# The input projection of an attention and convolution kernel: float32 matmuls replaced by three f32r products of high and low parts

## The chip, the cores and the metric

One core of one Trainium2 chip runs the kernel. The metric is the device time in microseconds (us). Six names are used for the engines: PE (TensorE, matmul), PEld (its weight load), DVE (VectorE), ACT (ScalarE), POOL (GpSimd) and SP (SyncE, which issues the DMAs here).

## The reference, cut to what matters

```python
# x: (16, 512, 1024) f32; mask = cond_2048: (16, 1024) of 0 and 1; 8 heads of 64
q      = x^T @ Wq.T                                # (16, 1024, 512)
qh     = q split into 8 heads
scores = (1/8) * einsum('bhqd,bhkd->bhqk', qh, qh) # queries, keys and values are all qh
logits = (scores * cmask + (1 - cmask) * -1e30) * rmask
ctx    = softmax(logits) @ qh
x      = x + (ctx @ Wo.T)^T
x      = x + causal_depthwise_conv(x, taps = cond_2048) + bias
```

## The kernel before, in words

The attention goes batch by batch, 16 in all: batch 0 and batch 15 are written out ("first" and "last"), the 14 between are one hardware loop ("mid"). A batch is four pairs p of heads, a pair two heads i, a head eight steps t of 128 keys. The order is written by hand, engine by engine, with semaphores; on top of a step's own work a table (`MAX_AT`, `PROJ_AT`, `OUT_AT` and others) says which extra pieces a step carries.

**A step** of a head, (p, i, t): PE makes the scores of 128 keys against 1024 queries (L509 and L510, four matmuls into `sc`). ACT takes the exponentials in two halves (L627, into `p32`, two buffers) and rounds them to f32r (L629, `phi`, four buffers). POOL makes the remainder `plo = p32 - phi` (L699). PE multiplies `phi` and `plo` with the values two steps later (L523 and L527, six matmuls into `pv`). The scores of step t+1 wait for the exponentials of step t; the exponentials of step t wait for the `plo` of step t-2, since `p32` has two buffers; `phi` and `plo` wait for the products of step t-4.

**The extra pieces** share two banks `misc`: the maxima of the next head's scores (L471 on PE, L743 on DVE), their transpose `mneg` (L484, L763) at step 5, the values' transpose (L478, evicted by ACT L604) at step 6, the output projection of the batch before (L495, DVE L788), and the input projection. The last stands at steps 0 and 1 of a pair's first head and is for the next pair: at (3, 0) it is for pair 0 of the next batch. It multiplies `wq` and `xb`, both float32, over four blocks of 128 rows (L457); ACT evicts it twice (L593, `lo`; L594, `hi`), and DVE makes from it `mhi`, `lo` and `mlo` at steps 2 and 3 (L731, L726, L734). DVE normalises a pair at step 5 of the next pair's second head (`ct`, L779).

**The queue of SP** moves these rows to their places with DMAs (`operands`, `operands2`: L332), brings `mneg` as one row of 4 KB into `quer2` (`rows`: L362), and loads x. A head's first scores wait for its `mneg` row (`s_rows`). x and the mask of the next batch, 2 MB and 512 KB, are loaded by `load_x` (L323, L324), which waits for `s_masked`, that is `mlo` of the batch's last pair. In the kernel before the call stands at the beginning of head (2, 1):

```python
if phase != "last" and (p, i) == (2, 1):
    load_x(b + 1, pair(b, 3) + 1)
if i == 0 and not end:
    operands(*next_pair(b, p))
```

After the attention comes the convolution (L923 to L1014), which the change does not touch.

Of the kernel before, what the change touches and what calls it, by code (L numbers as in the profile page):

```python
# [15 lines left out]
P = 128  # L16
# [6 lines left out]
BAND = 96  # L23
NP32, NPHI, NPLO = 2, 4, 4
LAG = 2

# [89 lines left out]
class Prelude:  # L116
# [3 lines left out]
    def __init__(self, nc, ctx):  # L120
# [6 lines left out]
        with ExitStack() as place:  # L127
            self.keys = sb("keys", [P, 4, T], F32R, place)
            self.quer = sb("quer", [P, 4, T], F32R, place)
        self.xin = sb("xin0", [P, SLOTS, TH], F32)  # L130
        with ExitStack() as place:
# [3 lines left out]
        with ExitStack() as place:  # L135
            self.phi = sb("phi", [P, NPHI, T], F32R, place)
            self.plo = sb("plo", [P, NPLO, T], F32R, place)
            self.p32 = sb("p32", [P, NP32, T], F32, place)
        with ExitStack() as place:
# [4 lines left out]
        self.brow = sb("brow", [P, T], BF16)  # L144
        self.own = sb("own", [P, CH], F32)
        self.tri = sb("tri", [P, 2, CH], F32)
# [37 lines left out]
def build_attention(nc, x, cond, wqT, woT, x1, pre, taps_in, bias):  # L184


    with ExitStack() as ctx:  # L187
        def sb(name, shape, dt):
            return ctx.enter_context(nc.sbuf_tensor(name, shape, dt))

# [5 lines left out]

        wq = sb("wq", [P, DT, D], F32)
# [3 lines left out]
        xb = sb("xb", [P, DT, T], F32)  # L201
        mask = sb("mask", [P, T], F32)
# [9 lines left out]
        keys, quer, keys2, quer2 = pre.keys, pre.quer, pre.keys2, pre.quer2  # L212
        val = sb("val", [P, 2, KT, 2, P], F32R)
        mrow = sb("mrow", [P, KT], F32)
        mneg = sb("mneg", [KT, P], F32R)
        mask8r = sb("mask8r", [KT, P], F32R)
# [3 lines left out]
        ct = sb("ct", [P, PAIRS, T], F32)  # L220
        xo = sb("xo", [P, 2, T], F32)

# [7 lines left out]
        s_ident = sem("s_ident")  # L230
        s_x = sem("s_x")
        s_mask8 = sem("s_mask8")
        s_off8 = sem("s_off8")
# [76 lines left out]
        def tok(t):  # L310
            return slice(t * P, (t + 1) * P)

        x_v = x.rearrange("b (k p) t -> b p k t", p=P)
        cond_v = cond.rearrange("b (o t) -> b o t", o=1)
# [4 lines left out]
        def _(sp):  # L319
            def load_x(b, staged):  # L320
                if staged is not None:
                    sp.wait_ge(s_masked, staged)
                sp.dma_start(xb[:], x_v[b]).then_inc(s_x, 16)  # L323
                sp.dma_start(mask[:], cond_v[b].to_broadcast([P, T])).then_inc(s_x, 16)  # L324
# [49 lines left out]
            def start():  # L374
                for s in s_xo_out:
                    sp.sem_inc(s, 16)
                wq_v = wqT.rearrange("(k p) e -> p k e", p=P)
                sp.dma_start(wq[:, :, 0:P], wq_v[:, :, 0:P]).then_inc(s_begin, 16)
                sp.dma_start(xb[:, :, half(0)], x_v[0][:, :, half(0)]).then_inc(s_begin, 16)
                sp.dma_start(xb[:, :, half(1)], x_v[0][:, :, half(1)]).then_inc(s_x, 16)  # L380
                sp.dma_start(mask[:], cond_v[0].to_broadcast([P, T])).then_inc(s_x, 16)
                load_mask8(0, None)
                sp.dma_start(wq[:, :, P:D], wq_v[:, :, P:D]).then_inc(s_const, 16)
# [56 lines left out]
        def _(pe):  # L440
# [6 lines left out]
            def project(phase, b, p, step, h):  # L447

                out, full = take(phase, b, step, ("proj", h))
                out = out[:, 0:HALF]  # L450
                nb, np_ = (b, p) if phase == "start" else next_pair(b, p)
                if phase == "start":
                    pe.wait_ge(*((s_begin, 32) if h == 0 else (s_x, 32)))
                elif h == 0 and np_ == 0:
                    pe.wait_ge(s_x, 32 * nb + 32)
                for k in range(DT):
                    last = pe.matmul(out, wq[:, k, np_ * P:(np_ + 1) * P], xb[:, k, half(h)],  # L457
                                     start=(k == 0), stop=(k == DT - 1))
                last.then_inc(full, 1)
# [84 lines left out]
            def start():  # L544
# [3 lines left out]
                do("start", 0, 0, "head", PHASES["start"]["head"], (0, 0, 0))  # L548
                pe.wait_ge(s_const, 32)

# [31 lines left out]
        def _(act):  # L582
# [48 lines left out]
            def do(phase, b, p, step, items, nxt):  # L631
                for item in items:
                    if item[0] == "proj":
                        high_part(phase, b, p, step, item[1])
                    elif item[0] == "vt":
                        values(phase, b, step, item, nxt)

            def start():
                do("start", 0, 0, "pair", PHASES["start"]["pair"], None)
                do("start", 0, 0, "head", PHASES["start"]["head"], (0, 0, 0))  # L640

            def batch(phase, b):
                for p in range(PAIRS):
                    for i in range(2):
                        for t in range(KT):
                            first = phase == "first" and p == 0 and i == 0
                            exponentials(b, p, i, t, first)
                            if t == LAG - 1 and not first:
                                copy_context(*((b, p, 0) if i == 1 else (*before(b, p), 1)))
# [9 lines left out]
        def _(pool):  # L659
# [42 lines left out]
            def start():  # L702
                constants()
                masks()

            def batch(phase, b):
                for p in range(PAIRS):
                    for i in range(2):
                        for t in range(KT):
                            split(b, p, i, t, phase == "first" and p == 0 and i == 0)  # L710

            run(pool, start, batch, lambda: None)

        @block.vector
        def _(dve):
# [76 lines left out]
            def do(phase, b, p, step, items, nxt):  # L792
                for item in items:
# [4 lines left out]
                    elif item[0] == "out":  # L798
                        residual(phase, b, step, item, b - 1, item[1] + 1)

            def start():
                constants()
                table_masks()
                for parts in STAGE_AT.values():
                    for part in parts:
                        stage(0, 0, part)
                do("start", 0, 0, "head", PHASES["start"]["head"], (0, 0, 0))

            def batch(phase, b):
                for p in range(PAIRS):  # L810
                    for i in range(2):
                        for t in range(KT):
# [5 lines left out]
                            if not (phase == "first" and p == 0):  # L818
                                for part in REC_AT.get((i, t), []):
                                    reciprocals(*before(b, p), part)  # L820
                                if (i, t) == NORM_AT:
                                    normalise(*before(b, p))

            def table_masks():
# [240 lines left out]
```

## Time and profile before

| | us |
|---|---|
| median of 3 runs | 4283.91 |
| lowest and highest | 4280.56, 4286.85 |
| the profiled execution | 4281.65 |
| its span in the trace | 4279.9 |
| PE busy | 4128.9 (96%) |
| PE weight load busy | 2721.4 (64%) |
| ACT busy | 2849.9 (67%) |
| POOL busy | 2595.8 (61%) |
| DVE busy | 2491.4 (58%) |

The profile is of one execution. Busy times of PE are modelled at their ends, since matmuls overlap: the distance from start to start of neighbouring matmuls tells more of their price than the duration of one. PEclk is the granted clock of TensorE, 1.00 for 2.4 GHz and 0.5 for 1.2 GHz. A line number L is that of the kernel before. In a timeline "x4" means four instructions merged into one row, and the bracket at a row's end tells how long the engine was idle before it and who released it.

### The profile page before, as it was taken

The page shows a single profiled execution, that of the slowest core. Times are in us where ns is not written, and L with a number is a line of the kernel's source. Part 1 is how long each engine was busy: PE and PEld are TensorE (multiplying, and loading weights), DVE is VectorE, ACT ScalarE, POOL GpSimd, SP SyncE. Part 2 cuts the span into 40 slices and gives each one's busy share as a digit, 9 for nine tenths or more (in the row PEclk, how much of TensorE's full clock was granted, in tenths as well). Part 3 has the DMA queues.
Part 4 walks back from the last instruction along what each step waited for, and adds up shares of the span by engine and source line. Part 5 has one row for each costly group of instructions (what it writes and reads, how often), then busy time and mean ns, then how long its engine had stood idle before and what let it go on. Part 6 is the DMA issues. An engine that isn't in the chain of part 4 may idle for free. (4 is left out here: it accounts for less than half of the span.)

```text
span 4279.9 us, 56952 instructions
## 1 busy us (share of the span) xinstructions
PE 4128.9 (96%) x18688; PEld 2721.4 (64%) x18688; DVE 2491.4 (58%) x2260; ACT 2849.9 (67%) x3905; POOL 2595.8 (61%) x1044
## 2 busy tenths in 40 slices
PE   7999999999999999999999999999999999999799
PEld 4665666666566666656666665666666566666598
DVE  4664555556455655655565565656556565656576
ACT  4775767667576766757676675767667575767465
POOL 4775757667575766757576675757667575766300
PEclk8999999999999999999999999999999999999899
DMA  3323333232333333233333323333332332332488
GB/s 104 82 67 71 80 82 94 71 88 65 74 80 79 94 74 85 65 77 80 77 94 75 84 69 76 81 74 94 75 84 70 74 83 71 94 74 60 128 285 268
DMA packets 286191, 385.34 MB, mean 90 GB/s; under 512 B 148947, under 2 KB 217171, under 8 KB 285782
## 3 DMA queue, kind: packets, MB, share of 16 engines
q1 hardware_dynamic: 285910, 381.57, 34.9%
q8 instruction: 179, 2.93, 0.3%
q14 instruction: 102, 0.84, 0.1%
HBM read 112.28 MB, written 67.11 MB: 42 GB/s over the span
## 5 line engine op out<-in xcount | busy, mean ns | idle before, releaser
L699 POOL TENSOR_TENSOR plo<-p,phi 128x1024 fp32r<-128x1024 f32 x1024 | 2590.4, 2541 | 1404.1 <-ACT phi L629 1399.2
L743 DVE TENSOR_REDUCE mrow<-misc 128x1 f32<-128x1024 f32 x1024 | 1214.0, 1217 | 1067.5 <-PE misc L471 1067.5
L627 ACT ACTIVATE p<-sc 128x512 f32<-128x512 f32 x2048 | 1110.0, 594 | 855.2 <-PE sc L510 610.0
L523 PE MATMUL pv<-phi,val 128*128 128x512 f32 x4096 | 1192.3, 413 | 44.0 <-issue 44.0
L629 ACT ACTIVATE phi<-p 128x1024 fp32r<-128x1024 f32 x1024 | 1086.4, 1061 | 32.5
L523 PEld LDWEIGHTS pv<-phi,val 128*128 128x128 f32 x4096 | 724.1, 188 | 372.4 <-issue 226.0
L509 PE MATMUL sc<-quer,keys 128*128 128x512 f32 x2048 | 917.2, 448 | 23.5 <-issue 18.4
L510 PE MATMUL sc<-quer,keys 96*128 96x512 f32 x2048 | 808.6, 395 | 0.0
L527 PE MATMUL pv<-plo,val 128*128 128x512 f32 x2048 | 644.2, 395 | 0.7 <-POOL plo L699 0.7
L509 PEld LDWEIGHTS sc<-quer,keys 128*128 128x128 f32 x2048 | 386.7, 189 | 195.1 <-issue 75.7
L773 DVE RECIPROCAL den<-den 128x128 f32<-128x128 f32 x512 | 468.4, 935 | 50.2 <-ACT den L616 23.9
L495 PE MATMUL misc<-ct,wo 128*128 128x512 f32 x1024 | 466.9, 599 | 26.8 <-DVE mrow L743 18.9
L457 PE MATMUL misc<-xb,wq 128*128 128x512 f32 x1024 | 464.7, 597 | 8.7 <-DMA xb<-x 6.8
L510 PEld LDWEIGHTS sc<-quer,keys 96*128 96x128 f32 x2048 | 388.9, 190 | 112.0 <-issue 48.1
L471 PE MATMUL misc<-quer 64*128 64x512 f32 x2048 | 426.7, 465 | 25.0 <-DMA keys<-lo 11.7
L527 PEld LDWEIGHTS pv<-plo,val 128*128 128x128 f32 x2048 | 384.2, 188 | 93.5 <-POOL plo L699 1.4
L788 DVE TENSOR_TENSOR xo<-misc,xo 128x512 f32<-128x512 f32 x128 | 88.5, 691 | 450.8 <-PE misc L495 446.1
L471 PEld LDWEIGHTS misc<-quer 64*128 64x128 f32 x2048 | 167.3, 185 | 277.0 <-issue 244.2
L495 PEld LDWEIGHTS misc<-ct,wo 128*128 128x128 f32 x1024 | 189.7, 190 | 241.1 <-issue 204.6
L457 PEld LDWEIGHTS misc<-xb,wq 128*128 128x128 f32 x1024 | 195.3, 191 | 208.0 <-issue 187.0
L593 ACT ACTIVATE lo<-misc 128x512 f32<-128x512 f32 x128 | 76.6, 598 | 314.5 <-PE misc L457 314.5
L779 DVE TENSOR_TENSOR ct<-ca,den 128x1024 f32<-128x1024 f32 x63 | 205.4, 3260 | 13.9 <-DVE mneg L763 13.6
(67 smaller groups left out, 2647.7 us busy)
## 6 DMA issues: line engine op xcount, KB each, us to landing
keys<-hi SPq DMA_DIRECT2D x256, 256.0 KB, 3.1
quer<-mhi SPq DMA_DIRECT2D x256, 256.0 KB, 4.4
keys<-lo SPq DMA_DIRECT2D x128, 256.0 KB, 4.9
quer<-mlo SPq DMA_DIRECT2D x128, 256.0 KB, 3.8
xo<-x SPq DMA_DIRECT2D x64, 512.0 KB, 4.0
x<-xo SPq DMA_DIRECT2D x64, 512.0 KB, 5.1
xin<-x SPq DMA_DIRECT2D x16, 2048.0 KB, 13.6
out<-stage SPq DMA_DIRECT2D x64, 512.0 KB, 6.4
```

The source lines that it names most:

```text
L457: last = pe.matmul(out, wq[:, k, np_ * P:(np_ + 1) * P], xb[:, k, half(h)], start=(k == 0), stop=(k == DT - 1))
L471: last = pe.matmul(out[:, half(h)], quer[rows, k, tok(q)], quer[rows, k, half(h)], start=True, stop=True)
L495: last = pe.matmul(out, wo[:, k, m * P:(m + 1) * P], ct[:, k, half(h)], start=(k == 0), stop=(k == PAIRS - 1))
L509: pe.matmul(sc[:, h, :], keys[:, k, tok(t)], quer[:, k, half(h)], start=True, stop=False)
L510: pe.matmul(sc[:, h, :], keys2[:, i, tok(t)], quer2[:, i, half(h)], start=False, stop=True).then_inc(s_sc, 1)
L523: pe.matmul(pv[:, half(h)], val[:, i, t, part, :], phi[:, t % NPHI, half(h)], start=(t == 0 and part == 0), stop=False)
L527: last = pe.matmul(pv[:, half(h)], val[:, i, t, 0, :], plo[:, t % NPLO, half(h)], start=False, stop=(t == KT - 1))
L627: act.activation(p32[:, t % NP32, half(h)], sc[:, h, :], ACT.Exp, scale=SCALE).then_inc(s_p32, 1)
L629: act.activation(phi[:, t % NPHI, :], p32[:, t % NP32, :], ACT.Copy).then_inc(s_phi, 1)
L699: pool.tensor_tensor(plo[:, t % NPLO, :], p32[:, t % NP32, :], phi[:, t % NPHI, :].bitcast(F32), ALU.subtract).then_inc(s_plo, 1)
L743: reduced = dve.tensor_reduce(mrow[:, q:q + 1], misc[:, k, :], AX.X, ALU.max)
L773: dve.reciprocal(d, d).then_inc(s_rden, 1)
```

## The change

A float32 matmul of the input projection gives way to three f32r matmuls. The weights and x are split on the chip: ACT rounds a copy to f32r (`wqh`, `xh`), and the remainder is a subtraction (`wql`, `xl`). The projection is the sum `wqh*xh + wql*xh + wqh*xl`, twelve matmuls where the four float32 ones stood; the product of the two low parts is left out.

The weights are split at the start of the kernel. x of batch b+1 is split during head (2, 1) of batch b, in four blocks of 128x1024: ACT makes the high parts at steps 2, 3, 4 and 5, POOL the low parts of blocks 0 and 1 behind its `plo` of steps 4 and 6, DVE those of blocks 2 and 3 at steps 6 and 7. The projection at (3, 0) step 0 waits for all four. `load_x` is called at head (2, 0), after the `operands` of that head and ahead of `rows`. Some buffers change places in SBUF (`val`, `mneg` and `mask8r` move into the prelude's space, and the raw weights lie in `ct`).

```diff
+HI_AT = {2: 0, 3: 1, 4: 2, 5: 3}
+LO_POOL = {4: 0, 6: 1}
+LO_DVE = {6: [2], 7: [3]}
...
-                        if phase != "last" and (p, i) == (2, 1):
-                            load_x(b + 1, pair(b, 3) + 1)
                         if i == 0 and not end:
                             operands(*next_pair(b, p))
+                        if phase != "last" and (p, i) == (2, 0):
+                            load_x(b + 1, pair(b, 3) + 1)
                         if not (end and i == 1):
                             rows(nb, np_, ni)
...
                 if phase == "start":
-                    pe.wait_ge(*((s_begin, 32) if h == 0 else (s_x, 32)))
+                    if h == 0:
+                        pe.wait_ge(s_wql, 1)
+                    pe.wait_ge(s_xl, h + 1)
                 elif h == 0 and np_ == 0:
-                    pe.wait_ge(s_x, 32 * nb + 32)
-                for k in range(DT):
-                    last = pe.matmul(out, wq[:, k, np_ * P:(np_ + 1) * P], xb[:, k, half(h)],
-                                     start=(k == 0), stop=(k == DT - 1))
+                    pe.wait_ge(s_xl, split_done(nb, 2, 2))
+                    pe.wait_ge(s_xl_pool, 2 * nb)
+                cols = slice(np_ * P, (np_ + 1) * P)
+                for n, (w, xs) in enumerate(((wqh, xh), (wql, xh), (wqh, xl))):
+                    for k in range(DT):
+                        last = pe.matmul(out, w[:, k, cols], xs[:, k, half(h)],
+                                         start=(n == 0 and k == 0), stop=(n == 2 and k == DT - 1))
...
+            def input_high(b, k):
+
+                if k == 0:
+                    act.wait_ge(s_x, 32 * b + 32)
+                act.activation(xh[:, k, :], x32[:, k, :], ACT.Copy).then_inc(s_xh, 1)
...
             def start():
+                act.wait_ge(s_begin, 32)
+                act.activation(wqh[:, :, 0:P], wq32[:, :, 0:P], ACT.Copy).then_inc(s_wqh, 1)
+                act.activation(xh[:, :, half(0)], x32[:, :, half(0)], ACT.Copy).then_inc(s_xh, 1)
+                act.wait_ge(s_x, 32)
+                act.activation(xh[:, :, half(1)], x32[:, :, half(1)], ACT.Copy).then_inc(s_xh, 1)
...
+            def input_low(b, k):
+
+                pool.wait_ge(s_xh, split_done(b, DT, k + 1))
+                pool.tensor_tensor(xl[:, k, :], x32[:, k, :], xh[:, k, :].bitcast(F32), ALU.subtract).then_inc(s_xl_pool, 1)
...
+            def first_low(h):
+
+                dve.wait_ge(s_xh, h + 1)
+                dve.tensor_tensor(xl[:, :, half(h)], x32[:, :, half(h)], xh[:, :, half(h)].bitcast(F32), ALU.subtract).then_inc(s_xl, 1)
```

Three places show how the order moves. The first is SP's queue in head (2, 0) of the loop, from the last operand rows of pair 3 on. Before:

```order
L332 DMA keys<-lo 64x1024 x2
L361 REGISTER_ALU
L362 DMA quer<-mneg 1x8x128
L370 REGISTER_ALU
L371 ISA
L371 DMA x<-xo 128x16x64
L350 ISA
L332 DMA keys<-hi 64x1024
L332 DMA quer<-mlo 64x1024
L323 ISA
L323 DMA xb<-x 128x4x1024
```

And of the change (L383 is the `mneg` row, L344 and L345 the load):

```order
L353 DMA keys<-lo 64x1024 x2
L344 ISA
L344 DMA x<-x 128x4x1024
L345 ISA
L345 DMA mask<-cond 128x1024
L382 REGISTER_ALU
L383 DMA quer<-mneg 1x8x128
L391 REGISTER_ALU
L392 ISA
L392 DMA x<-xo 128x16x64
```

The load of x and the mask now stand ahead of the `mneg` row of head (2, 1) in the same queue, where they stood behind it.

The second place is POOL in head (2, 1) of the change, from step 4 to step 7 (L741 is the `plo` of a step, L751 the low part of x); before, only the `plo` stood there:

```order
L741 TENSOR_TENSOR plo<-p,phi 128x1024
L750 ISA
L751 TENSOR_TENSOR xl<-x,xh 128x1024
L738 REGISTER_ALU
L741 TENSOR_TENSOR plo<-p,phi 128x1024
L738 REGISTER_ALU
L741 TENSOR_TENSOR plo<-p,phi 128x1024
L750 REGISTER_ALU
L751 TENSOR_TENSOR xl<-x,xh 128x1024
L738 REGISTER_ALU
L741 TENSOR_TENSOR plo<-p,phi 128x1024
```

Between the `plo` of step 4 and that of step 7 POOL now has four instructions where it had two.

The third place is DVE in the same head, from step 5 on (L812 is `mneg`, L828 is `ct`, L863 the low part of x, L792 a maximum of the head after):

```order
L812 SCALAR_TENSOR_TENSOR mneg<-misc,mask 8x128
L827 REGISTER_ALU
L828 TENSOR_TENSOR ct<-ca,den 128x1024
L862 REGISTER_ALU
L863 TENSOR_TENSOR xl<-x,xh 128x1024
L862 REGISTER_ALU
L863 TENSOR_TENSOR xl<-x,xh 128x1024
L789 REGISTER_ALU
L792 TENSOR_REDUCE mrow<-misc 128x1 x2
```

Two subtractions over two SBUF operands now follow `ct`, where the next head's maxima followed it.

## Rows read from the trace of the kernel before

**Rows 1.** The page: busy time of each engine, its share of the span

```profile
PE 4128.9 (96%) x18688; PEld 2721.4 (64%) x18688; DVE 2491.4 (58%) x2260; ACT 2849.9 (67%) x3905; POOL 2595.8 (61%) x1044
```

**Rows 2.** The attention as one stretch: us, busy of PE, PEld, DVE, ACT, POOL, PEclk

```profile
40.00:3930.00 3890.00, 3796.35 (x15098) 2442.91 (x15099) 2238.13 (x2018) 2647.89 (x3628) 2531.53 (x1001) 1.00 0.32 78
```

**Rows 3.** PE in order of time: start us, us, line; float32, then f32r matmuls

```profile
2074.79 3.60 PE L457 MATMUL misc<-xb,wq 128*128 128x512 f32 x8
2078.23 3.60 PE L495 MATMUL misc<-ct,wo 128*128 128x512 f32 x8
...
2173.29 0.39 PE L509 MATMUL sc<-quer,keys 128*128 128x512 f32 x1
...
2174.22 1.09 PE L523 MATMUL pv<-phi,val 128*128 128x512 f32 x4
```

**Rows 4.** A group of the page: the input projection

```profile
L457 PE MATMUL misc<-xb,wq 128*128 128x512 f32 x1024 | 464.7, 597 | 8.7 <-DMA xb<-x 6.8
```

**Rows 5.** The line of the load of x: count, first and last start

```profile
L323 SPq DMA_DIRECT2D xb<-x x15: 455/460/632, 188.3 to 3676.6; - x15
```

**Rows 6.** ACT in head (2, 1), in order of time: phi of step 2, exponentials of step 3

```profile
2191.20 1.06 ACT L629 ACTIVATE phi<-p 128x1024 fp32r<-128x1024 f32 x1
2192.28 1.08 ACT L627 ACTIVATE p<-sc 128x512 f32<-128x512 f32 x2
```

**Rows 7.** POOL, in order of time, in heads (2, 0) and (2, 1)

```profile
2168.08 13.91 POOL L699 TENSOR_TENSOR plo<-p,phi 128x1024 fp32r<-128x1024 f32 x5 [4.38 <-ACT phi L629]
...
2192.42 4.75 POOL L699 TENSOR_TENSOR plo<-p,phi 128x1024 fp32r<-128x1024 f32 x2 [2.19 <-ACT phi L629]
...
2200.69 5.76 POOL L699 TENSOR_TENSOR plo<-p,phi 128x1024 fp32r<-128x1024 f32 x2 [0.79 <-ACT phi L629]
```

**Rows 8.** DVE at the same times: lo, mlo and ct

```profile
2168.02 1.22 DVE L726 TENSOR_TENSOR lo<-lo,hi 128x1024 fp32r<-128x1024 f32 x1
...
2170.29 2.28 DVE L734 TENSOR_TENSOR mlo<-lo,mask 128x1024 fp32r<-128x1024 f32 x1
...
2200.92 3.25 DVE L779 TENSOR_TENSOR ct<-ca,den 128x1024 f32<-128x1024 f32 x1 [0.23 <-DVE mneg L763]
```

**Rows 9.** PE: the first scores of head (2, 1), the projection at (3, 0)

```profile
2181.33 0.50 PE L509 MATMUL sc<-quer,keys 128*128 128x512 f32 x1
...
2208.77 3.59 PE L457 MATMUL misc<-xb,wq 128*128 128x512 f32 x8
```

**Rows 10.** SP's queue in head (2, 0)

```profile
2171.26 2.34 SPq L332 DMA_DIRECT2D keys<-lo  x2
2176.23 0.71 SPq L362 DMA_DIRECT2D quer<-mneg  x1
```

**Rows 11.** Stretches of 1 and 6 us: busy per engine, PEclk, DMA share, GB/s

```profile
2176.00:2177.00 1.00, 1.00 (x6) 0.77 (x5) 0.85 (x2) 0.97 (x2) 1.00 (x1) 1.00 0.22 41
2184.00:2190.00 6.00, 5.33 (x24) 3.35 (x22) 6.00 (x7) 5.05 (x6) 5.82 (x3) 1.00 0.98 396
```

**Rows 12.** Start of the kernel, DMA issues: KB each, median us to landing

```profile
wq<-wqT SPq DMA_DIRECT2D x1, 768.0 KB, 9.2
```

**Rows 13.** Start of the kernel, in order of time

```profile
3.81 0.40 SPq L383 DMA_DIRECT2D wq<-wqT  x1
...
6.85 8.71 PE L457 MATMUL misc<-xb,wq 128*128 128x512 f32 x16 [6.85 <-DMA xb<-x]
...
39.30 0.63 SPq L362 DMA_DIRECT2D quer<-mneg  x1
...
41.19 0.76 PE L509 MATMUL sc<-quer,keys 128*128 128x512 f32 x1 [3.44 <-DMA quer<-mneg]
```

**Rows 14.** The tail of the attention, PE after an idle stretch, in order of time

```profile
3982.51 1.47 PE L523 MATMUL pv<-phi,val 128*128 128x512 f32 x4 [2.17 <-issue]
```

**Rows 15.** The stretch right after it: busy per engine, PEclk, DMA share, GB/s

```profile
3983.00:3987.00 4.00, 4.00 (x12) 3.13 (x12) 0.00 (x0) 2.60 (x5) 3.21 (x2) 0.57 0.00 0
```

**Rows 16.** A wait of PE in one batch, 1932 to 2181 us: total, times, longest

```profile
PE sc L509 <- issue: 1.4, 1, 1.4
```

More of the change, by code:

```diff
@@ L129, in __init__ @@
             self.quer = sb("quer", [P, 4, T], F32R, place)
+            self.mneg = sb("mneg", [KT, P], F32R, place)
+            self.mask8r = sb("mask8r", [KT, P], F32R, place)
         self.xin = sb("xin0", [P, SLOTS, TH], F32)
@@ L187, in build_attention, with sb @@
     with ExitStack() as ctx:
-        def sb(name, shape, dt):
-            return ctx.enter_context(nc.sbuf_tensor(name, shape, dt))
+        def sb(name, shape, dt, where=ctx):
+            return where.enter_context(nc.sbuf_tensor(name, shape, dt))
         def ps(name, shape):
@@ L200, in build_attention @@
         ident = ident_r[:].bitcast(F32)
-        xb = sb("xb", [P, DT, T], F32)
+        xh = sb("xh", [P, DT, T], F32R)
+        with ExitStack() as place:
+            x32 = sb("x32", [P, DT, T], F32, place)
+        xl = sb("xl", [P, DT, T], F32R)
         mask = sb("mask", [P, T], F32)
@@ L212, in build_attention @@
         keys, quer, keys2, quer2 = pre.keys, pre.quer, pre.keys2, pre.quer2
-        val = sb("val", [P, 2, KT, 2, P], F32R)
+        val = pre.val
         mrow = sb("mrow", [P, KT], F32)
-        mneg = sb("mneg", [KT, P], F32R)
-        mask8r = sb("mask8r", [KT, P], F32R)
+        mneg, mask8r = pre.mneg, pre.mask8r
         p32, phi, plo = pre.p32, pre.phi, pre.plo
@@ L231, in build_attention @@
         s_x = sem("s_x")
+        s_wq = sem("s_wq")
+        s_wqh = sem("s_wqh")
+        s_wql = sem("s_wql")
+        s_xh = sem("s_xh")
+        s_xl_pool = sem("s_xl_pool")
+        s_xl = sem("s_xl")
         s_mask8 = sem("s_mask8")
@@ L311, in tok, with split_done @@
             return slice(t * P, (t + 1) * P)
+        def split_done(b, per, of):
+            return 2 + per * (b - 1) + of
         x_v = x.rearrange("b (k p) t -> b p k t", p=P)
@@ L647, in batch @@
                             exponentials(b, p, i, t, first)
+                            if phase != "last" and (p, i) == (2, 1) and t in HI_AT:
+                                input_high(b + 1, HI_AT[t])
                             if t == LAG - 1 and not first:
@@ L710, in batch @@
                             split(b, p, i, t, phase == "first" and p == 0 and i == 0)
+                            if phase != "last" and (p, i) == (2, 1) and t in LO_POOL:
+                                input_low(b + 1, LO_POOL[t])
             run(pool, start, batch, lambda: None)
@@ L799, in do, with weights_low, input_low @@
                         residual(phase, b, step, item, b - 1, item[1] + 1)
+            def weights_low(part, cols):
+                dve.wait_ge(s_wqh, part + 1)
+                dve.tensor_tensor(wql[:, :, cols], wq32[:, :, cols], wqh[:, :, cols].bitcast(F32), ALU.subtract).then_inc(s_wql, 1)
+            def first_low(h):
+                dve.wait_ge(s_xh, h + 1)
+                dve.tensor_tensor(xl[:, :, half(h)], x32[:, :, half(h)], xh[:, :, half(h)].bitcast(F32), ALU.subtract).then_inc(s_xl, 1)
+            def input_low(b, k):
+                dve.wait_ge(s_xh, split_done(b, DT, k + 1))
+                dve.tensor_tensor(xl[:, k, :], x32[:, k, :], xh[:, k, :].bitcast(F32), ALU.subtract).then_inc(s_xl, 1)
             def start():
@@ L803, in start @@
                 table_masks()
+                weights_low(0, slice(0, P))
+                first_low(0)
+                first_low(1)
                 for parts in STAGE_AT.values():
@@ L822, in batch @@
                                     normalise(*before(b, p))
+                            if phase != "last" and (p, i) == (2, 1):
+                                for k in LO_DVE.get(t, []):
+                                    input_low(b + 1, k)
             def table_masks():
```

24 lines of the change are left out of this document (16 added, 8 removed).

## The prediction

> **What bounds the kernel now.** I read the busy times of the page first, then the attention as one stretch, then PE in order of time, then one batch in the places that the change touches. The page has PE at 96% and no other engine above 67% [rows 1]. In the stretch of the attention PE is busy 3796 of 3890 us [rows 2], so a matmul taken away there shortens the kernel, as long as nobody else is late. Busy time alone could mislead, since PE's durations overlap; so look at starts. Four f32r matmuls of 512 columns go from 2173.29 to 2174.22, that is 0.2325 us each. The eight instructions of one projection (four float32 matmuls, each counted twice) stand 3.44 us before what follows them [rows 3]. PE really is full, and the steps show which others could become late: the scores of a step wait for exponentials, these wait for `plo` two steps back, and POOL makes that.
>
> **What the change takes from PE.** A projection becomes 12 x 0.2325 = 2.79 us, 0.65 less. There are 1024 / 8 = 128 projections [rows 4], two of them at the start, before the stream of work is full. The other 126 give 126 x 0.645 = 81.3 us, all on the path if the other engines keep up. The shape and kind are those of the rows, so this price is firm; at 0.25 us a matmul, more than the four of the row take, the gain would be 55 us.
>
> **The splitting of x, 15 times** [rows 5]. Take the batch whose head (2, 1) begins at 2181 us. *ACT*: `phi` of step 2 ends at 2192.3. A copy of 1024 columns costs what `phi` costs, 1.06, and the exponentials of a step 1.08 [rows 6]. With a copy behind each step, the high part of block 0 ends at 2193.3, step 3 with its copy at 2196.5, and `phi` of step 4 is ready at 2198.7. *POOL and DVE*: here the rows show something that the busy shares hide. DVE's subtraction takes 1.22 us alone, but `mlo` took 2.28 and `ct` 3.25 [rows 8]; and POOL's `plo`, 2.37 in an undisturbed pair, took 13.91 for five over `lo` and `mlo`, and 5.76 for two over `ct` [rows 7]. So a DVE instruction with two SBUF operands and a POOL one don't run together: each waits for the other, and every such meeting costs POOL 5.76 - 4.75 = 1.0 us. From 2198.7 these two therefore have one queue: `plo` 4, low part of block 0, `ct`, `plo` 5, low part 2, `plo` 6, low part 3, low part of block 1. That is 5 x 2.37 + 3 x 1.0 = 14.9 us, to 2213.6, plus 0.2 for the semaphore. The projection at (3, 0), which must wait for the low parts, began at 2208.77 [rows 9]. It is 5.0 us late, whatever order the two engines take in between: `plo` 5 is late too and holds up exponentials and PE at step 7, but inside the same 5 us. Nothing later gives it back, since PE is then the bound again. 15 x 5.0 = **75 us**. Bounds: were the meetings free, the queue is 11.9 us and the delay about 2; were every wait of step 7 in addition, 7.
>
> **The load, moved by half a head.** Before, the load stood behind the `mneg` row of head (2, 1); now it is ahead of it, issued at about 2173.6 when `keys<-lo` has been issued, where `mneg` comes at 2176.23 [rows 10]. Do DMAs of this queue overtake each other? At the start 768 KB were issued at 3.81 [rows 13] and landed 9.2 us later [rows 12]; at the 396 GB/s of a load under way [rows 11] 768 KB take 2 us. They waited for what was ahead of them. I take it that 4 KB wait as well. The operand rows ahead drain until about 2176.2 (the DMA share falls to 0.22 in that microsecond [rows 11]). 2.62 MB then take 6.3 to 6.6 us, and with 0.4 to the semaphore the row lands at about 2183.1, where the first scores of head (2, 1) started at 2181.33 [rows 9]. That is 1.8 us of idle PE, 15 x 1.8 = **27 us**. Bounds: 0 if small transfers pass (the row lands 1.9 us after its issue on an empty queue, 39.30 to 41.19 [rows 13]), 3 if the load is slow to start. All of the head shifts, so this adds to the 5.0.
>
> **The start.** PE's first projection began at 6.85 [rows 13], on landing. Now ACT must copy 512 columns and then 2048 (0.6 + 2.0 by its 1.06 for 1024), DVE subtract 2048 (2 x 1.22): PE begins at 11.8. Before, 16 instructions took 8.71 where 16 x 0.43 = 6.9 would do, so 1.8 us went to the low clock; 24 x 0.2325 + 1.8 = 7.4, to 19.2 instead of 15.56: **+3.7 us**. The split of the remaining weights (1536 columns, 1.4 on ACT and 1.8 on DVE) falls where DVE idles for the operand rows, and costs nothing; without that cover it would be 1.8, once. The changed SBUF places cost nothing that a row could show.
>
> **The clock.** In the tail PE was idle for 2.17 us, and in the 4 us after it the granted clock was 0.57 [rows 14, 15]; four matmuls then lasted 1.47 where they last 1.09 at full clock [rows 3]. At half rate for most of 4 us that is 1.7 us lost. In the loop no idle stretch was that long (the longest of a batch is 1.4 us [rows 16]), and there the clock stayed at 1.00 [rows 2]. Now PE idles 2 to 4 us in head (2, 1) and before (3, 0). Part of the slow stretch lies under the wait for the low parts, so I take 1 us of the 0 to 1.7: **+15 us**. The Trainium skill (TensorE: Matmul & The Clock Gate, "HAM oscillation — how this bites in real kernels") speaks of the same danger, a clock that falls in each wait between groups of matmuls and is paid every time; by it the sum would have the full 1.7, 26 us, and by the loop of the trace alone 0.
>
> **The sum.** 4281.65 - 81.3 + 75 + 27 + 3.7 + 15 = 4321. The profiled execution is 2.3 us below the median, so I say **4323**. A measurement of this kernel can tell 0.2%, 8.6 us, from no change; this is 0.9% slower.
>
> **Rivals.**
> *Faster: the cover holds.* PE's 81 us are certain, and both costs are worked out from queues. If the meetings of POOL and DVE don't add up in that head (the delay is then the 2 us of the lower bound) and small rows pass the load, the time is 4281.65 - 81 + 30 + 4 = 4234, with the median 4237; with the DMA wait as forecast, 4264. For it: POOL is 61% busy and idles whenever projections run. Against it: the extra work sits in steps 4 to 7, the steps without projections, where POOL has `plo` every 2.4 us. It decides at a delay of 3.7 us per batch, both waits together. Chance 0.18.
> *No change: no DMA wait and no fall of the clock.* The 5.0 stay: 4281.65 - 81.3 + 75 + 3.7 = 4279, with the median 4281. For it: the load might reach the engines before the operand rows have drained. Chance 0.12.
> *Much slower: the clock.* If it falls after each of the two waits of a batch and neither slow stretch lies under a wait, that is 15 x 3.4 = 51 instead of 15: 4357, with the median 4359. For it the row of the tail, and beside it the skill's section named above. Against it: the idle stretches of the loop, up to 1.4 us, never did it. Chance 0.12.
> *The change does not do what it says*, that is, x comes no earlier: excluded by the order rows, the load is three DMAs earlier.
> The forecast has 0.58. Its own range is 4300 to 4345.
>
> **How the numbers follow.** Slower by over 0.2%: 0.58 + 0.12 = 0.70. Within: 0.12. Faster: 0.18. The range reaches down to 4258, taking in no change and the milder half of the faster case, and up to 4355, which leaves out the rest of the clock case.
>
> **What would show it.** Right: projections of 2.8 us; in each batch but the last, PE idle 1.5 to 2 us at the start of head (2, 1), put down to the `mneg` DMA; PE waiting for `plo` at step 7, and the projection at (3, 0) waiting for POOL's or DVE's `xl`, 5 us in all; the distance from load to load 249 to 251 us, where it was (3676.6 - 188.3) / 14 = 249.2 [rows 5]; PE busy down by some 80 us, idle up by more. The steps are wrong if the scores of (2, 1) start without a wait (then the order of the queue), if `plo` in steps 4 to 7 keeps its 2.4 us beside the low parts (then the shared queue of POOL and DVE), or if the granted clock stays at 1.00 through the loop (then the 15 us).

## The result and the profile after

The changed kernel takes 4365.93 us (median; 4350.04 to 4366.11), the kernel before, run beside it, 4283.86 (4280.56 to 4286.85). The ratio is 1.018, with an interval from 1.0166 to 1.0194: 1.8% slower, where 0.9% was forecast. The profiled execution took 4350.04. It is the shortest of them, so what the trace shows may be up to 16 us short. A fourth execution took 10689.9 us; it is left out of the range and the ratio, and without it the median is 4365.75.

The page of the changed kernel, the line of busy times, beside [rows 1]:

```profile
PE 4092.9 (94%) x19200; PEld 2841.2 (65%) x19200; DVE 2599.0 (60%) x2294; ACT 2909.8 (67%) x3969; POOL 2701.4 (62%) x1074
```

PE is busy 36 us less in a kernel that is 68 us longer (4350.04 against the 4281.65 of the execution profiled before). The work was taken away, and idle time and slow time came in. The groups of the changed lines, beside [rows 4]:

```profile
L741 POOL TENSOR_TENSOR plo<-p,phi 128x1024 fp32r<-128x1024 f32 x1024 | 2612.4, 2562 | 1366.9 <-ACT phi L656 1360.8 <-PE pv L553 3.1
L483 PE MATMUL misc<-xh,wqh 128*128 128x512 f32 x512 | 142.8, 401 | 42.5 <-POOL xl L751 28.9 <-DVE xl L858 11.7 <-DVE mrow L792 1.9
L863 DVE TENSOR_TENSOR xl<-x,xh 128x1024 fp32r<-128x1024 f32 x30 | 100.7, 3396 | 0.0
L751 POOL TENSOR_TENSOR xl<-x,xh 128x1024 fp32r<-128x1024 f32 x30 | 86.1, 2869 | 0.0
L669 ACT ACTIVATE xh<-x 128x1024 fp32r<-128x1024 f32 x60 | 62.5, 1042 | 0.0
```

DVE's low part takes 3.40 us on average, where the same subtraction alone takes 1.22 [rows 8]; POOL's takes 2.87 where 2.37 is its own price [rows 7]. The waits of PE name the places:

```profile
PE sc L535 <- DMA quer<-mneg: 54.1, 15, 5.1
PE misc L483 <- POOL xl L751: 28.9, 15, 2.6
PE pv L553 <- POOL plo L741: 19.2, 16, 1.3
PE misc L483 <- DVE xl L858: 11.7, 1, 11.7
```

The first three have 15 or 16 places each, about one per batch, and are 102 us together. Of the first row 3.4 us are the wait at the start of the kernel, which was there before [rows 13]; the other 51 are new, 3.6 us in each of 14 batches (in batch 0 PE stands idle for 1.8 us at this point, which the profile puts down to "issue"). The fourth row is the start. The distance from one load of x to the next is now (3734.0 - 180.1) / 14 = 253.9 us, where it was 249.2 [rows 5]:

```profile
L344 SPq DMA_DIRECT2D x<-x x15: 375/438/524, 180.1 to 3734.0; - x15
```

Now one batch in order of time. SP's queue, which answers to [rows 10]:

```profile
2206.03 2.34 SPq L353 DMA_DIRECT2D keys<-lo  x2
2208.57 0.43 SPq L344 DMA_DIRECT2D x<-x  x1
2209.18 1.01 SPq L345 DMA_DIRECT2D mask<-cond  x1
2210.88 0.71 SPq L383 DMA_DIRECT2D quer<-mneg  x1
```

The row is issued 2.3 us after the load that stands ahead of it. PE at the start of head (2, 1), which answers to the first row of [rows 9]:

```profile
2215.34 0.62 PE L553 MATMUL pv<-plo,val 128*128 128x512 f32 x2
2218.94 0.79 PE L535 MATMUL sc<-quer,keys 128*128 128x512 f32 x1 [2.97 <-DMA quer<-mneg]
2219.52 0.63 PE L536 MATMUL sc<-quer,keys 96*128 96x512 f32 x1
...
2222.08 2.07 PE L549 MATMUL pv<-phi,val 128*128 128x512 f32 x4
2223.95 1.05 PE L553 MATMUL pv<-plo,val 128*128 128x512 f32 x2
2224.81 0.63 PE L535 MATMUL sc<-quer,keys 128*128 128x512 f32 x1
...
2247.66 0.50 PE L535 MATMUL sc<-quer,keys 128*128 128x512 f32 x1
```

PE begins 8.1 us after the row's issue, having idled for 2.97. Then four matmuls last 2.07 us where they last 1.09 at full clock [rows 3], and scores of two matmuls stand 0.43 apart (2219.52 to 2219.95 in the trace), not 0.23. The stretches around it (us, busy of PE, PEld, DVE, ACT, POOL, PEclk, DMA share, GB/s) show what the clock did:

```profile
2211.00:2217.00 6.00, 4.97 (x27) 3.78 (x25) 2.58 (x3) 5.49 (x8) 5.67 (x3) 1.00 0.98 369
2217.00:2219.00 2.00, 0.06 (x1) 0.07 (x1) 0.00 (x0) 0.56 (x1) 1.36 (x1) 0.89 1.13 336
2219.00:2225.00 6.00, 6.00 (x15) 3.93 (x16) 3.21 (x3) 2.25 (x3) 3.10 (x2) 0.50 0.65 128
2225.00:2250.00 25.00, 22.94 (x102) 15.68 (x101) 19.61 (x14) 21.31 (x28) 18.63 (x8) 0.99 0.10 22
```

In this batch PE works for 6 us at 1.2 GHz, the lower of its two levels, after 3 us of idling, and then at 2.4 GHz again. The end of the head, from the wait for `plo` at step 7 to the projection at (3, 0), which answers to the second row of [rows 9]:

```profile
2246.93 0.73 PE L553 MATMUL pv<-plo,val 128*128 128x512 f32 x2 [1.23 <-POOL plo L741]
...
2253.56 1.20 PE L483 MATMUL misc<-xh,wqh 128*128 128x512 f32 x4 [2.43 <-POOL xl L751]
2254.59 1.07 PE L483 MATMUL misc<-xh,wql 128*128 128x512 f32 x4
2255.50 1.08 PE L483 MATMUL misc<-xl,wqh 128*128 128x512 f32 x4
2256.42 0.39 PE L535 MATMUL sc<-quer,keys 128*128 128x512 f32 x1
```

The projection now takes 2256.42 - 2253.56 = 2.86 us where it took 3.44 [rows 3], but it stands 34.6 us behind the head's first scores where it stood 27.4 [rows 9]. POOL in the 13 us before it, beside [rows 7]:

```profile
2241.18 2.40 POOL L751 TENSOR_TENSOR xl<-x,xh 128x1024 fp32r<-128x1024 f32 x1
2243.54 6.68 POOL L741 TENSOR_TENSOR plo<-p,phi 128x1024 fp32r<-128x1024 f32 x2
2250.18 3.33 POOL L751 TENSOR_TENSOR xl<-x,xh 128x1024 fp32r<-128x1024 f32 x1
```

And DVE at the same times, beside [rows 8]:

```profile
2241.32 3.34 DVE L828 TENSOR_TENSOR ct<-ca,den 128x1024 f32<-128x1024 f32 x1 [0.23 <-DVE mneg L812]
2244.58 6.72 DVE L863 TENSOR_TENSOR xl<-x,xh 128x1024 fp32r<-128x1024 f32 x2
2251.22 2.34 DVE L792 TENSOR_REDUCE mrow<-misc 128x1 f32<-128x1024 f32 x2
```

The two take turns: POOL's instructions stand 3.3 us apart, 1.0 more than its own 2.37, and DVE's 3.35, which is a POOL instruction and its own work. The start, beside [rows 13]:

```profile
11.69 2.05 PE L483 MATMUL misc<-xh,wqh 128*128 128x512 f32 x4 [11.69 <-DVE xl L858]
...
45.48 0.77 PE L535 MATMUL sc<-quer,keys 128*128 128x512 f32 x1 [3.45 <-DMA quer<-mneg]
```

PE begins 4.8 us later, and the first scores are 4.3 us later than before.

So the trace holds all that was forecast, and more of it. Three questions stay for experiments: what each part costs by itself, since 82 us of loss are the small difference of large terms; whether the position of the load alone does what the wait says; and whether the full projection can be had without its costs.

### The profile page after: what moved, and what is told of

The parts are those of the page before. It is cut to its first block and busy times, and to the rows that moved or that the text cites. A ratio compares the mean times of both kernels' runs of the same rounds, so it can differ in the third digit from the quotient of the medians.

```text
span 4348.3 us, 58190 instructions
## 1 busy us (share of the span) xinstructions
PE 4092.9 (94%) x19200; PEld 2841.2 (65%) x19200; DVE 2599.0 (60%) x2294; ACT 2909.8 (67%) x3969; POOL 2701.4 (62%) x1074
## 5 line engine op out<-in xcount | busy, mean ns | idle before, releaser
L741 POOL TENSOR_TENSOR plo<-p,phi 128x1024 fp32r<-128x1024 f32 x1024 | 2612.4, 2562 | 1366.9 <-ACT phi L656 1360.8
L792 DVE TENSOR_REDUCE mrow<-misc 128x1 f32<-128x1024 f32 x1024 | 1213.5, 1216 | 1043.6 <-PE misc L497 1043.6
L549 PE MATMUL pv<-phi,val 128*128 128x512 f32 x4096 | 1212.0, 418 | 43.6 <-issue 43.6
L549 PEld LDWEIGHTS pv<-phi,val 128*128 128x128 f32 x4096 | 736.1, 191 | 382.2 <-issue 234.3
L535 PE MATMUL sc<-quer,keys 128*128 128x512 f32 x2048 | 877.8, 429 | 75.7 <-DMA quer<-mneg 54.1
L553 PE MATMUL pv<-plo,val 128*128 128x512 f32 x2048 | 646.2, 397 | 19.2 <-POOL plo L741 19.2
L521 PE MATMUL misc<-ct,wo 128*128 128x512 f32 x1024 | 466.9, 599 | 27.4 <-DVE mrow L792 19.5
L828 DVE TENSOR_TENSOR ct<-ca,den 128x1024 f32<-128x1024 f32 x63 | 206.7, 3281 | 13.9 <-DVE mneg L812 13.6
L483 PE MATMUL misc<-xh,wqh 128*128 128x512 f32 x512 | 142.8, 401 | 42.5 <-POOL xl L751 28.9
L642 ACT ACTIVATE ca<-pv 64x1024 f32<-64x1024 f32 x128 | 130.8, 1022 | 41.3 <-PE pv L553 40.2
```

The costliest lines, as they stand in the source:

```text
L521: last = pe.matmul(out, wo[:, k, m * P:(m + 1) * P], ct[:, k, half(h)], start=(k == 0), stop=(k == PAIRS - 1))
L535: pe.matmul(sc[:, h, :], keys[:, k, tok(t)], quer[:, k, half(h)], start=True, stop=False)
L549: pe.matmul(pv[:, half(h)], val[:, i, t, part, :], phi[:, t % NPHI, half(h)], start=(t == 0 and part == 0), stop=False)
L553: last = pe.matmul(pv[:, half(h)], val[:, i, t, 0, :], plo[:, t % NPLO, half(h)], start=False, stop=(t == KT - 1))
L741: pool.tensor_tensor(plo[:, t % NPLO, :], p32[:, t % NP32, :], phi[:, t % NPHI, :].bitcast(F32), ALU.subtract).then_inc(s_plo, 1)
L792: reduced = dve.tensor_reduce(mrow[:, q:q + 1], misc[:, k, :], AX.X, ALU.max)
```

## The experiments

Medians are in us. A ratio is to the kernel before, run on the same chip in the same hour, with its interval. "Clock" is the granted clock over a whole execution: 0.993 before, 0.981 with the change.

### The load behind the row, the change else untouched

```diff
                             operands(*next_pair(b, p))
-                        if phase != "last" and (p, i) == (2, 0):
-                            load_x(b + 1, pair(b, 3) + 1)
                         if not (end and i == 1):
                             rows(nb, np_, ni)
+                        if phase != "last" and (p, i) == (2, 0):
+                            load_x(b + 1, pair(b, 3) + 1)
```

> The change with one edit: in head (2, 0) the load of x and the mask is issued behind the mneg row and not ahead of it. Theory (the row waits in the queue behind 2.6 MB, 54 us in all, and the idle PE then brings the clock down): the wait for mneg at the first scores of head (2, 1) goes, and with it the slow stretch behind it, 2.5 us a batch; 4366 - 54 - 38 = about 4275, between 4265 and 4295. Rival (the loss is the split of x in head (2, 1), the wait for the row only moves PE's idle time ahead of it): the 54 us turn up again as waits for POOL, and the time stays above 4340.

Measured: 4280.5 (4276.55 to 4284.35), ratio 0.9993 (0.9984 to 1.0003), clock 0.988. The waits of PE:

```profile
PE misc L483 <- POOL xl L751: 35.0, 15, 2.4
PE pv L553 <- POOL plo L741: 19.2, 16, 1.2
PE sc L535 <- DMA quer<-mneg: 3.4, 1, 3.4
```

Only the start still waits for the row. The order of two issues was worth 4365.9 - 4280.5 = 85 us, 5.7 per batch. The trace explains 51 of it as wait. The clock's share can be bounded: 0.981 against 0.988 over 4350 us is 30 us at most. Together that is 81. The forecast had 27 for the row and 15 for all of the clock.

### The same order in the kernel before

```diff
-                        if phase != "last" and (p, i) == (2, 1):
-                            load_x(b + 1, pair(b, 3) + 1)
                         if i == 0 and not end:
                             operands(*next_pair(b, p))
+                        if phase != "last" and (p, i) == (2, 0):
+                            load_x(b + 1, pair(b, 3) + 1)
                         if not (end and i == 1):
                             rows(nb, np_, ni)
```

> The kernel before with one edit: the load of x and the mask moved to where the change has it, in head (2, 0) ahead of the mneg row; float32 projection and no split. Theory (order in the queue): PE waits 3 to 4 us in each of 15 batches for mneg, 54 us, and loses 2 us more each by the clock, 4284 + 54 + 30 = about 4368. Rival (the wait needs the faster projection, or the load alone is harmless): within 10 us of 4284.

Measured: 4379.57 (4378.92 to 4384.44), ratio 1.0229 (1.0212 to 1.0246), clock 0.982: 96 us slower with no split and no new matmul at all.

```profile
PE sc L509 <- DMA quer<-mneg: 63.2, 15, 4.7
```

So the cost belongs to the place of the load and not to the rest of the change. Without the 3.4 us of the start the wait is 4.3 us per batch, longer than the 3.6 of the changed kernel. PE arrives at that point equally late in both, 5.0 and 5.1 us after the issue of the row; the row lets PE go 9.3 us after its issue on average, against 8.7. Why it takes longer here is open.

### Is the lead needed? The load at its old place

```diff
+                        if phase != "last" and (p, i) == (2, 1):
+                            load_x(b + 1, pair(b, 3) + 1)
                         if i == 0 and not end:
                             operands(*next_pair(b, p))
-                        if phase != "last" and (p, i) == (2, 0):
-                            load_x(b + 1, pair(b, 3) + 1)
```

> The change with the load where the kernel before had it, at the start of head (2, 1). The load takes 9.6 us to land and the first high part is due 11 us after the head's start. Theory: no wait for mneg, and x lands just in time, so the same as with the load behind the row, 4265 to 4295; the half head of lead is not needed. Rival (x lands too late, its split is pushed towards the projection that needs it): 3 us and more a batch slower than with the load behind the row, over 4315.

Measured: 4282.64 (4276.96 to 4287.83), ratio 0.9996 (0.9986 to 1.0006). That is the time of the first experiment within the spread of either. The half head of lead bought nothing; ACT's first copy at step 2 finds x in time in either case.

### The low parts left out

From the first experiment's kernel. The low parts of x are not made inside the loop; the third product reads `xh` again, so PE has the same twelve matmuls, and waits for the high parts only. Left out is the correction `wqh*xl`.

```diff
-LO_POOL = {4: 0, 6: 1}
-LO_DVE = {6: [2], 7: [3]}
+LO_POOL = {}
+LO_DVE = {}
...
-                    pe.wait_ge(s_xl, split_done(nb, 2, 2))
-                    pe.wait_ge(s_xl_pool, 2 * nb)
+                    pe.wait_ge(s_xh, split_done(nb, DT, DT))
...
-                    for n, (w, xs) in enumerate(((wqh, xh), (wql, xh), (wqh, xl))):
+                    for n, (w, xs) in enumerate(((wqh, xh), (wql, xh), (wqh, xh))):
```

> As with the load behind the mneg row (4280.5), and without the low parts of x from batch 1 on: the four subtractions of a batch are left out, the third product takes the high part of x again, and the projection at (3, 0) waits for the high parts alone. The matmuls are as many. Theory (the queue that POOL and DVE share makes the projection 4.6 to 5 us late in each of 15 batches): 62 to 75 us less than 4280.5, about 4212. Rival (ACT's four copies are what is late): less than 25 us below 4280.5.

Measured: 4214.79 (4210.94 to 4218.71), ratio 0.9841 (0.9824 to 0.9857), clock 0.991. The low parts cost 4280.5 - 4214.8 = 66 us, 4.4 per batch. The forecast for the queue shared by POOL and DVE was 75. In the first experiment the two waits they cause are 35.0 + 19.2 = 54 us, and 0.991 against 0.988 is at most 13 more. Of the waits of this kernel one row bears on the next experiment:

```profile
PE sc L534 <- ACT p L653: 6.1, 15, 0.4
```

### No split inside the loop

In addition the high parts are left out (`HI_AT = {}`; PE waits for x itself). Only batch 0 is projected from its own x, the others from what batch 0 left; PE's work is the same.

```diff
-HI_AT = {2: 0, 3: 1, 4: 2, 5: 3}
+HI_AT = {}
...
-                    pe.wait_ge(s_xh, split_done(nb, DT, DT))
+                    pe.wait_ge(s_x, 32 * nb + 32)
```

> As the kernel without low parts, and without ACT's four copies of a batch too: batches 1 to 15 are projected from the high part of batch 0, with all the matmuls and the load of x. It shows what the twelve f32r matmuls give alone. Theory: 81 us below the kernel before and 4 us for the start back, about 4206, and within 15 us of the kernel that still makes the high parts. Rival (the saving on PE is smaller than 0.645 us a projection, since other engines bound the steps with projections): over 4230.

Measured: 4201.71 (4197.55 to 4205.21), ratio 0.981 (0.9794 to 0.9826), clock 0.991. This is the bare effect of the cheaper projection with its longer start: -82 us, where -81.3 + 3.7 = -77.6 was forecast. ACT's 60 copies cost 4214.8 - 4201.7 = 13 us, 0.9 per batch, where the forecast had nothing. The row above is half of it: with the copies the scores wait 0.4 us for exponentials once a batch, and without them this row is gone. The other half has no row.

### All low parts on DVE

From the first experiment's kernel.

```diff
-LO_POOL = {4: 0, 6: 1}
-LO_DVE = {6: [2], 7: [3]}
+LO_POOL = {}
+LO_DVE = {3: [0], 4: [1], 6: [2], 7: [3]}
...
-                    pe.wait_ge(s_xl, split_done(nb, 2, 2))
-                    pe.wait_ge(s_xl_pool, 2 * nb)
+                    pe.wait_ge(s_xl, split_done(nb, 4, 4))
```

> As with the load behind the mneg row (4280.5), but all four low parts on DVE (steps 3, 4, 6 and 7 of head (2, 1)) and none on POOL. Theory (a low part on POOL holds the shared queue for 2.4 us, one on DVE costs POOL 1.0): the queue is 2 x 1.4 = 2.8 us shorter, of which 1.5 to 2.8 reach the projection; 4238 to 4258. Rival (it doesn't matter who makes them, the number of instructions counts; or DVE, with its maxima, becomes the late one): 4275 or more.

Measured: 4291.53 (4284.61 to 4300.18), ratio 1.0017 (1.0007 to 1.0027). The theory missed: it should have been at least 22 us faster than the first experiment and is 11 slower. The rival's second half came true, that DVE, with its maxima, becomes the late one:

```profile
2200.34 1.16 DVE L862 TENSOR_TENSOR xl<-x,xh 128x1024 fp32r<-128x1024 f32 x1
...
2204.78 2.44 DVE L862 TENSOR_TENSOR xl<-x,xh 128x1024 fp32r<-128x1024 f32 x1
...
2210.48 6.71 DVE L862 TENSOR_TENSOR xl<-x,xh 128x1024 fp32r<-128x1024 f32 x2
2217.11 2.34 DVE L791 TENSOR_REDUCE mrow<-misc 128x1 f32<-128x1024 f32 x2
```

The same instruction lasts 1.16 us where POOL stands idle as it begins and 3.36 where POOL has one `plo` behind the other, behind `ct` at steps 6 and 7. The maxima that stand behind it are late in their turn. They hold the banks `misc` that the projection needs, and the projection begins only after them:

```profile
2218.45 1.47 PE L482 MATMUL misc<-xh,wqh 128*128 128x512 f32 x4 [3.67 <-DVE mrow L791]
```

The wait has moved from POOL's row to DVE's, 57.4 us in 17 places. What counts is thus less which engine makes the low parts than at which step.

### The low parts on DVE, one step earlier

```diff
-HI_AT = {2: 0, 3: 1, 4: 2, 5: 3}
-LO_POOL = {4: 0, 6: 1}
-LO_DVE = {6: [2], 7: [3]}
+HI_AT = {1: 0, 3: 1, 4: 2, 5: 3}
+LO_POOL = {}
+LO_DVE = {2: [0], 3: [1], 5: [2], 6: [3]}
```

The rest is as in the experiment before. All four low parts, and the first high part, stand one step earlier.

> As with all low parts on DVE, but spread: high parts at steps 1, 3, 4 and 5, low parts at steps 2, 3, 5 and 6 of head (2, 1), so that the first meetings with POOL fall where it has slack. Theory (the lateness builds up in steps 4 to 7, where POOL has a plo every 2.4 us): 1.2 to 1.5 us a batch remain of the 5, time 4220 to 4232, 1.3% under the kernel before. Rival (the sum of POOL's and DVE's work counts, not its place): within 8 us of the kernel with all low parts on DVE at steps 3, 4, 6 and 7.

Measured: 4229.32 (4223.4 to 4233.13), ratio 0.9867 (0.9851 to 0.9884), clock 0.992. It computes all that the changed kernel computes and beats both: 1.3% less than before and 137 us less than the change.

```profile
L862 DVE TENSOR_TENSOR xl<-x,xh 128x1024 fp32r<-128x1024 f32 x60 | 130.0, 2186 | 2.6 <-ACT xh L668 2.6
```

```profile
PE misc L482 <- DVE mrow L791: 10.7, 17, 2.8
```

The low part has come down to 2.19 us on average, from 2.60 in the experiment before, and the wait for the maxima from 57.4 to 10.7. Over the kernel without low parts it costs 4229.3 - 4214.8 = 14 us where the change paid 66.

### Fewer bytes ahead of the row

From the changed kernel: only x (2 MB) stays ahead of the row, the mask (512 KB) goes behind it.

```diff
                 sp.dma_start(x32[:], x_v[b]).then_inc(s_x, 16)
+
+            def load_mask(b):
                 sp.dma_start(mask[:], cond_v[b].to_broadcast([P, T])).then_inc(s_x, 16)
...
                             rows(nb, np_, ni)
+                        if phase != "last" and (p, i) == (2, 0):
+                            load_mask(b + 1)
```

> The change with 2 MB (x) ahead of the mneg row as before and the 512 KB of the mask behind it. Theory (the row waits for the bytes ahead of it in its queue): 512 KB are 1.25 us at 410 GB/s, so the wait of PE at head (2, 1) falls from 3.6 to 2.3 us a batch, 35 us in all instead of 54; with a little less of the slow clock the time is 4366 - 19 - 5 = 4342, between 4325 and 4352. Rival (any large load ahead costs the same, or the row lands with the end of the whole burst): still 54 us of waiting, 4360 or more.

Measured: 4334.79 (4331.56 to 4340.63), ratio 1.0127 (1.011 to 1.0144).

```profile
PE sc L539 <- DMA quer<-mneg: 39.5, 15, 3.4
```

The wait follows the bytes: 3.6 us per batch with 2.62 MB ahead, 2.6 with 2.10 MB. The missing 0.52 MB are worth 1.3 us at the 396 GB/s of a load under way [rows 11], and 1.0 was measured. In both kernels the row is issued 2.3 to 2.4 us after the load and PE arrives 5.1 us after the row's issue, so a fixed cost of the issue would not have moved.

### The load from another queue

From the changed kernel: ACT's queue issues the load, at step 4 of head (2, 0), so that nothing stands ahead of the row in SP's.

```diff
-                        if phase != "last" and (p, i) == (2, 0):
-                            load_x(b + 1, pair(b, 3) + 1)
...
+                            if phase != "last" and (p, i, t) == (2, 0, 4):
+                                act.wait_ge(s_masked, pair(b, 3) + 1)
+                                act.dma_start(x32[:], x_v[b + 1]).then_inc(s_x, 16)
+                                act.dma_start(mask[:], cond_v[b + 1].to_broadcast([P, T])).then_inc(s_x, 16)
```

> The change with the load of x and the mask issued by ACT, at step 4 of head (2, 0), so at nearly the same time but in ACT's queue; the mneg row stays in SP's. Theory (the wait is one of order within a queue): the row passes, PE waits under 1 us a batch for it, 4280 to 4300, as with the load behind the row. Rival (the 16 engines are simply full, and the row waits for them whatever its queue): 2 to 4 us a batch of waiting for mneg, 4340 to 4366.

Measured: 4304.0 (4299.61 to 4313.87), ratio 1.0055 (1.0039 to 1.0072).

```profile
PE sc L533 <- DMA quer<-mneg: 24.3, 15, 3.4
```

It came out between the two expectations. Without the 3.4 us of the start PE waits 1.5 us per batch. The row no longer waits for the whole load: PE goes on 6.6 us after its issue on average, against 8.7 behind the load. But it is still late, beside a load that keeps the same DMA engines full. Which part of the row's way is slowed (its write, its read, its semaphore) this run doesn't tell. The order in one queue removes the wait altogether, so the other queue is the poorer cure.

## Why the prediction was right or wrong

The sign was right, and each mechanism that the forecast priced was there. The time was 4365.9, above the forecast of 4323 and above the range, whose upper end was 4355. The experiments, taken as a staircase from the kernel before, give each step its measured price (each difference of two medians, good to some 3 us, the last to less, since the three executions of the changed kernel lie 16 us apart):

```
step                                   forecast   measured   from
cheaper projection and longer start      -77.6       -82     no split in the loop, against before
ACT's copies                                0        +13     low parts left out, against no split
low parts on POOL and DVE                 +75        +66     first experiment, against low parts left out
load ahead of the mneg row                +27 }      +85     the change, against first experiment
clock, forecast as one term               +15 }
```

The miss is 43 us. It lies in two terms that were sized too small, the wait for the row (27, measured 51) and the clock (15, measured 45 to 52), and in one that was put at nothing, ACT's copies (13). The first two steps of the staircase that were forecast, projection and low parts, came out 13 us better and hid part of it. The steps +66 and +85 both hold a share of the clock, the first 13 us at most, so the low parts without it cost 53 us or more where 75 were forecast.

**The projection: right.** A projection takes 2.86 us at full clock where 2.79 was worked out. At the start the delay was 4.3 us, not 3.7: PE began at 11.69 (11.8 was forecast) but its slow stretch cost a little more.

**The shared queue of POOL and DVE: the mechanism was right, and the size nearly.** The step said 5 x 2.37 + 3 x 1.0 from `plo` 4 on, 5.0 us late per batch. POOL's five instructions from `plo` 4 to the second low part were to take 14.9 us; in the batch shown they go from 2238.81 to 2253.47, which is 14.7. Of the 34.6 - 27.4 = 7.2 us by which the projection has moved, 2.6 are the slow clock at the head's start (below), which leaves 4.6. The staircase says 4.4, or 5.3 with ACT's copies, which stood ahead of this queue.

**The row behind the load: the mechanism was right, the size wrong.** The term "1.8 us of idle PE, 15 x 1.8 = 27 us" measured 3.6 in 14 batches, 51 us in the profiled execution. The working had the row land 2183.1 - 2176.23 = 6.9 us after its issue, and PE arrive 5.1 us after it. PE did arrive then; the row came 8.1 us after its issue in the batch shown, and 7.9 to 10.2 in the 14 batches, 8.7 on average. A part of this is the load's start, in which less was moved:

```profile
2211.00:2212.00 1.00, 1.00 (x6) 0.83 (x5) 1.00 (x2) 0.85 (x1) 0.99 (x2) 1.00 0.81 242
2212.00:2217.00 5.00, 3.97 (x23) 2.96 (x21) 1.58 (x2) 4.64 (x7) 4.68 (x2) 1.00 1.02 395
```

Once under way it has the rate that was assumed, but from 2211 on it moves 369 GB/s on average, by which 2.62 MB take 7.1 us and not 6.3 to 6.6. The upper bound of 3 was passed too, with waits up to 5.1. The run with fewer bytes ahead shows that the wait grows with the load's length, and the one with the load in ACT's queue that 1.5 of the 3.6 us need no order in a queue. What makes the row 1 us later in one batch than in the next is open.

**The clock: the mechanism was right, the size wrong.** The forecast took 1 us "of the 0 to 1.7" per batch because part of the slow stretch was to lie under the wait for the low parts. The slow stretch behind the row doesn't: the clock is low from PE's return on, or soon after it, and back up within 8 us, over 20 us before the low parts are due. In the batch shown the first step of the head takes 2224.81 - 2218.94 = 5.9 us. In the trace before, the same step took 2184.64 - 2181.33 = 3.3. That is 2.6 us lost, above the 1.7 that the tail had given as upper bound. Not every batch loses as much. Of two batches, the 8 us behind the wait:

```profile
1964.50:1972.50 8.00, 8.00 (x29) 5.30 (x30) 4.84 (x5) 4.29 (x6) 3.66 (x3) 0.79 0.52 97
2218.94:2226.94 8.00, 8.00 (x23) 5.07 (x24) 3.50 (x4) 3.41 (x6) 3.43 (x2) 0.60 0.50 98
```

Eight of the 15 batches are like the first (1.7 us of full clock lost), seven have a mean of 0.57 to 0.70 (2.4 to 3.4 us). Together that is 35 us. Later in the same heads the clock falls once more in 6 of the 15, which is another 10. Over the whole kernel the clock's loss is at most (0.993 - 0.981) x 4350 = 52 us. The rival "much slower: the clock" had 51 for it, with a slow stretch for each of the two waits, and its 4359 was closer than the forecast; the closeness of the time is partly luck, since the second fall came only in 6 batches, the first was dearer than its 1.7, and the row's term of 27 was as short there. Of the executions of the changed kernel one is 16 us faster than the two others at the same mean clock; since only that one was profiled, where these 16 us lie stays open.

**ACT's copies: wrong at nothing.** The forecast placed the copies behind each step's work and found no one waiting. They cost 0.9 us per batch, half of it in a row that names ACT's exponentials; where the other half lies isn't shown.

**The rivals on the fast side** needed POOL and DVE to run side by side or the row to pass the load. Neither happened. The saving they counted on was real: with both costs cut by order and timing, the kernel with the low parts on DVE one step earlier takes 4229, near the 4237 that this rival had worked out.

## What to carry to other kernels

A saving on the busiest engine is one number, and the places where its new inputs are made are many: place these by the neighbours' free steps, not by the engines' totals, since starting four subtractions and one copy a step earlier was worth 62 us here. Don't issue a large load ahead of a small row with a near deadline in the same queue; where the load isn't urgent, issue it behind. And count a new stall of PE of some 3 us twice, once as a wait and once for the slow clock behind it.

## What the runs showed of the hardware

- **Behind a wait of 3 us PE works for some microseconds at half its clock.** Behind an idle stretch of 2.97 us the granted clock was 0.50 for the whole stretch from 2219 to 2225. It fell behind all 14 waits of 2.9 to 5.1 us of the change, and behind the 1.8 us of its batch 0. With the mask behind the row it fell behind 10 of 14 waits of 1.6 to 3.0 us, and with the load in ACT's queue behind 1 of 14 of 1.0 to 2.3 us, one of 1.74 and not the longest. So between 1.6 and 3 us the length of the wait alone doesn't decide it. The Trainium skill (TensorE: Matmul & The Clock Gate, "HAM oscillation — how this bites in real kernels") describes a clock that falls again in every wait between groups of matmuls. The trace of the change agrees, and the full clock of the loop before [rows 2] shows that waits up to 1.4 us [rows 16] were harmless.
- **A DMA's queue isn't its only bound.** A 4 KB row behind 2.62 MB in one queue cost PE 3.6 us, behind 2.10 MB 2.6 us, and beside the same load in another queue still 1.5 us. The Trainium skill (DMA: Bandwidth & Descriptors, "Queues, rings and completion order") states that a DMA's semaphore increment lands only after every earlier write of the same DMA engine, across its queues. The 1.5 us would agree with that, but no run here separates it from engines that are simply full.
- **DVE pays more than POOL where the two take turns.** A subtraction of 128x1024 with two SBUF operands rose from 1.16 to 3.36 us on DVE, from 2.37 to 3.3 on POOL. The pair takes 3.35, nearly the 3.5 of both one after the other, so overlap gives almost nothing.
